# A new order at the start of a gated cross-attention kernel: second variances ahead, VectorE scales four tiles, x turned inside V's third product

## The reference

```python
x = x + tanh(g_xattn) * xattn(layernorm(x), ctx, mask, ...)
x = x + tanh(g_ffn) * ffn(layernorm(x), ...)
# xattn(h, ctx): 32 heads of 128
q = (rmsnorm(h) * ln_w) @ w_q.T ; k = ctx @ w_k.T ; v = ctx @ w_v.T
p = softmax(where(mask, q @ k.T + bias, -inf)) ; out = h + (p @ v) @ w_out.T
# ffn(h): h @ base_W.T plus 2 of 28 rank-8 experts, chosen by h @ gate_W.T
```

## Time and profile before

| | |
|---|---|
| median of 3 runs | 825.04 us |
| profiled execution, its own time | 824.99 us |
| its span | 823.2 us |
| TensorE busy | 812.8 us, 99% |
| VectorE, ScalarE, GpSimd busy | 592.9, 389.3, 454.0 us |

### The profile page before, as it was taken

One profiled execution on the slowest core, in us unless ns is written; L12 is line 12 of the kernel. 1 busy time (PEld: TensorE's weight loads), 2 busy tenths in 40 slices (PEclk: granted clock), 3 DMA queues, 4 the chain that ended last, 5 costly groups with the idle time before them and its releaser, 6 DMA issues.

```text
span 823.2 us, 14190 instructions
## 1 busy us (share of the span) xinstructions
PE 812.8 (99%) x4198; PEld 694.3 (84%) x4198; DVE 592.9 (72%) x1003; ACT 389.3 (47%) x1059; POOL 454.0 (55%) x418
## 2 busy tenths in 40 slices
PE   9979999999999999999999999999999999999998
PEld 8868888887878888888888888888888888888887
DVE  6796556766775445996888778877887788778752
ACT  6954444445222424565445634563555355545410
POOL 2465666666388383757754575457545754574200
PEclk9999999999999999999999999999999999999999
DMA  9457545454543835797566556655665565555002
GB/s 319 142 182 254 174 155 165 153 162 158 179 179 116 293 129 179 236 259 264 161 211 227 180 165 213 219 180 165 219 210 182 166 226 207 179 184 179 1 27 77
DMA packets 79102, 149.70 MB, mean 182 GB/s; under 512 B 8032, under 2 KB 42336, under 8 KB 77024
## 3 DMA queue, kind: packets, MB, share of 16 engines
q1 hardware_dynamic: 79072, 149.32, 54.4%
HBM read 97.91 MB, written 51.38 MB: 181 GB/s over the span
## 4 chain that ended last, share of the span: by engine, by line
PE 91%; DVE 4%; ACT 2%; POOL 1%; DMA 1%; issue 1%; SPq 0%; DVEq 0%; POOLq 0%; ACTq 0%
PE proj_ps L2075 18%; PE proj_ps L1895 13%; PE proj_ps L2137 11%; PE proj_ps L2156 8%; PE score_ps L1895 6%; PE proj_ps L1945 5%; PE score_ps L2156 4%; PE score_ps L1914 3%; PE proj_ps L2341 2%; PE pv_ps L2137 2%; PE turn_ps L2137 2%; PE pv_ps L2156 2%; PE turn_ps L2156 2%; PE pv_ps L1914 2%; PE turn_ps L1914 2%; PE score_ps L1945 1%
## 5 line engine op out<-in xcount | busy, mean ns | idle before, releaser
L664 POOL TENSOR_TENSOR comb<-mask_add,bias_sb 128x1024 f32<-128x1024 f32 x32 | 78.3, 2468 | 145.1 <-DVE attn L1642 145.1
L906 ACT ACTIVATE attn<-attn,neg_max 128x128 f32<-128x128 f32 x256 | 99.2, 390 | 37.8 <-DVE neg_max L1631 37.7
L1161 ACT ACTIVATE w_hi<-w_raw 128x256 fp32r<-128x256 f32 x105 | 40.0, 413 | 100.1 <-POOL w_raw L755 75.2
L765 POOL TENSOR_TENSOR w_lo<-w_raw,w_hi 128x256 fp32r<-128x256 f32 x105 | 74.4, 751 | 1.8 <-ACT w_hi L1161 1.8
L1664 DVE TENSOR_TENSOR acc<-proj_ps,acc 128x512 f32<-128x512 f32 x70 | 48.1, 689 | 35.6 <-PE proj_ps L1895 35.6
L717 POOL TENSOR_TENSOR w_lo<-w_raw,w_hi 128x256 fp32r<-128x256 f32 x64 | 49.9, 783 | 25.1 <-ACT w_hi L1021 24.9
L1895 PE MATMUL proj_ps<-w_hi,tf_hi 128*128 128x512 f32 x156 | 61.1, 392 | 0.0
L1895 PE MATMUL proj_ps<-w_hi,tf_lo 128*128 128x512 f32 x156 | 60.7, 389 | 0.0
L1895 PE MATMUL proj_ps<-w_lo,tf_hi 128*128 128x512 f32 x156 | 60.7, 389 | 0.0
L660 POOL TENSOR_TENSOR w_lo<-w_raw,w_hi 128x1024 fp32r<-128x1024 f32 x19 | 45.7, 2410 | 16.1 <-ACT w_hi L892 16.1
L1457 DVE TENSOR_TENSOR w_lo<-w_raw,w_hi 128x256 fp32r<-128x256 f32 x48 | 35.2, 738 | 24.5 <-ACT w_hi L1016 24.1
(11 more groups left out here) (414 smaller groups left out, 2526.9 us busy)
## 6 DMA issues: line engine op xcount, KB each, us to landing
w_raw<-in_weights SPq DMA_DIRECT2D x50, 512.0 KB, 5.6
q_spill<-attn SPq DMA_DIRECT2D x64, 256.0 KB, 3.1
qt<-q_spill SPq DMA_DIRECT2D x16, 1024.0 KB, 4.8
v_sb<-v_spill SPq DMA_DIRECT2D x32, 512.0 KB, 3.8
block_spill<-block_sb SPq DMA_DIRECT2D x30, 512.0 KB, 3.5
attn<-block_spill SPq DMA_DIRECT2D x120, 128.0 KB, 3.0
w_raw<-in_v_weights SPq DMA_DIRECT2D x18, 512.0 KB, 4.4
v_spill<-v_sb SPq DMA_DIRECT2D x16, 512.0 KB, 4.8
```

Source lines behind the costliest of these rows:

```text
L664: pool.tensor_tensor(comb[:, j, :, :], mask_add[:, :, :], bias_sb[:, j:j + 1, :].to_broadcast([P, B, S]), ALU.add).then_inc(comb_done, 1)
L765: pool.tensor_tensor(columns(w_lo, slot, n), raw, columns(w_hi, slot, n).bitcast(F32), ALU.subtract).then_inc(k_lo, 1)
L906: e = act.activation(probs[:, u, i, :], probs[:, u, i, :], ACT.Exp, bias=neg_max[:, u, i:i + 1], accum_out=row_sum[:, u, i:i + 1])
```

## The change

- GpSimd: the second root comes right behind the first, ahead of V's third rest, which no longer waits for the first shift; the sums for Q's pass 1 wait for three T rests instead of one product; kt's first rest moves from before pass 14 to behind the passes; the last V sums of group 0 move ahead of the fourth V weight sum of group 1.
- VectorE: the second variances come right behind the first shift; the second shift ahead of `norm_x(1)` to `(3)`; it scales tiles 4 to 7 itself; rests of the turned tiles and norms alternate in pairs; two rests of Q's A forms move behind `t_raw[3]`; `t_raw[2]` moves behind `rest_t(3)` and `rest_t(1)`.
- ScalarE: it no longer scales tiles 4 to 7, and its copies come in a new order; V's first two copies of the fourth product stand ahead of the first T form.
- TensorE: tiles 4 to 7 of x are turned in pairs inside V's third product and behind it.

```diff
--- before.py
+++ after.py
@@ -690,9 +690,8 @@
             early_rest(1)
             pool.wait_ge(consts_done, 3)
             inverse_root(1, slice(0, G), 2)
-            pool.wait_ge(shift_done, 1)
+            inverse_root(2, slice(G, B), 2)
             early_rest(2)
-            inverse_root(2, slice(G, B), 2)
             pool.wait_ge(shift_done, 2)
             early_rest(3)
 
@@ -726,7 +725,7 @@
 
             def q_phase(i):
                 if isinstance(i, int) and i == 0:
-                    pool.wait_ge(q_prod, 1)
+                    pool.wait_ge(t_lo_done, 3)
                 s_forms(i + 1)
                 rest_s(i + 1, 0, 0)
                 rest_s(i + 1, 1, 1)
@@ -736,8 +735,6 @@
             q_phase(0)
             with pool.Fori(1, NQ - 2) as i:
                 q_phase(i)
-            pool.wait_ge(kt_hi_done, 1)
-            pool.tensor_tensor(kt_form_at(1, 0), kt_raw[0], kt_form_at(0, 0).bitcast(F32), ALU.subtract).then_inc(kt_lo_done, 1)
             q_phase(NQ - 2)
 
             def rest_kt(n, place):
@@ -809,6 +806,8 @@
                 wait_v_lo(pool, g, 1)
                 pool.tensor_tensor(v_raw(g, R21), v_raw(g, R22), v_raw(g, R11), ALU.subtract).then_inc(v_sums, 1)
                 if g < VE:
+                    v_last_sums(g - 1)
+                if g < VE:
                     pool.wait_ge(vw_in[R12], 16 * (g + 1))
                 else:
                     wait_v_lo(pool, g, 2)
@@ -822,13 +821,15 @@
                     pool.wait_ge(v_post, g * VPOSTS + 9 + m)
                     pool.tensor_tensor(v_w[:, m, 0:VN[g]], v_w[:, m, 0:VN[g]], v_t[g][:, m, 0:VN[g]], ALU.add).then_inc(v_last, 1)
 
+            rest_kt(0, 1)
             rest_kt(1, 2)
             for g in range(1, VG):
                 if g >= VE:
                     v_rest(g, 0)
                 v_first_sums(g)
                 v_rest(g, 1)
-                v_last_sums(g - 1)
+                if g >= VE:
+                    v_last_sums(g - 1)
                 v_second_sums(g)
                 if g == 1:
                     pool.wait_ge(kt_lo_done, TF)
@@ -966,7 +967,7 @@
 
             def layer(i):
 
-                act.wait_ge(shift_done, i // G + 1)
+                act.wait_ge(shift_done, 1)
                 act.activation(acc[:, i, :], acc[:, i, :], ACT.Identity, bias=shift[:, i:i + 1], scale=root[:, 0, i:i + 1]).then_inc(acc_done, 1)
 
             early_half(0)
@@ -996,20 +997,17 @@
             act.activation(tanh_g[:, :], gates[:, :], ACT.Tanh).then_inc(tanh_done, 1)
             for i in range(G):
                 lead_xt(i)
-            layer(4)
-            layer(5)
+            raw_xt(0)
+            raw_xt(1)
             early_copy(2, 0)
-            raw_xt(0)
-            layer(6)
-            raw_xt(1)
-            early_copy(2, 1)
-            layer(7)
             raw_xt(2)
             raw_xt(3)
+            early_copy(2, 1)
+            lead_xt(4)
+            lead_xt(5)
             early_copy(2, 2)
             early_copy(2, 3)
-            lead_xt(4)
-            lead_xt(5)
+
             def lead_a(i, n, j, k):
 
                 wait_q_raw(act, i)
@@ -1027,24 +1025,21 @@
 
             act.wait_ge(ve_prod, 3 * VTILES)
             lead_a(0, 0, 0, 0)
+            lead_xt(6)
+            lead_xt(7)
+            early_copy(3, 0)
+            early_copy(3, 1)
+            lead_t(0)
+            lead_s(0, 0)
+            lead_s(0, 1)
+            lead_s(0, 3)
+            lead_s(0, 2)
             lead_a(0, 1, 0, 1)
             lead_a(0, 2, 1, 1)
-            lead_xt(6)
-            act.wait_ge(ve_prod, 2 * VTILES)
-            lead_s(0, 0)
-            lead_xt(7)
-            lead_t(0)
-            lead_s(0, 1)
-            early_copy(3, 0)
-            early_copy(3, 1)
             lead_t(1)
-            lead_s(0, 3)
-            lead_s(0, 2)
-            act.wait_ge(proj_done, UNITS)
             lead_t(3)
             early_copy(3, 2)
             early_copy(3, 3)
-            act.wait_ge(ve_prod, 4 * VTILES)
             lead_t(2)
 
             def lead_kt(n, place):
@@ -1420,21 +1415,24 @@
             x_stats(2)
             ordered(x_stats(3))
             layer_shift(1, first)
+            x_variances(1)
             rest_ctx(0, 1)
             rest_ctx(1, 1)
             dve.wait_ge(small_in, 48)
             norm_x(0)
-            norm_x(1)
             rest_ctx(2, 1)
             rest_ctx(3, 1)
-            norm_x(2)
-            norm_x(3)
-            x_variances(1)
             layer_shift(2, second)
-            for i in range(G):
+            for i in range(1, G):
+                norm_x(i)
+            dve.wait_ge(shift_done, 2)
+            for i in range(G, B):
+                dve.tensor_scalar(acc[:, i, :], acc[:, i, :], root[:, 0, i:i + 1], shift[:, i:i + 1], ALU.mult, ALU.add).then_inc(acc_done, 1)
+            for i in range(0, G, 2):
                 rest_xt(i, xt_hi_done, xt_lo_done, xn_ps)
-            for i in range(G, B):
-                norm_x(i)
+                rest_xt(i + 1, xt_hi_done, xt_lo_done, xn_ps)
+                norm_x(G + i)
+                norm_x(G + i + 1)
 
 
             def tile_ps(i, k):
@@ -1467,8 +1465,6 @@
             rest_xt(4, xt_hi_done, xt_lo_done, xn_ps)
             rest_xt(5, xt_hi_done, xt_lo_done, xn_ps)
             rest_a(0, 0, 0, 0)
-            rest_a(0, 1, 0, 1)
-            rest_a(0, 2, 1, 1)
             first_difference(6)
             first_difference(7)
             for i in range(G, B):
@@ -1477,9 +1473,11 @@
             rest_t(0, 1)
             dve.wait_ge(t_done, 2 * G)
             dve.tensor_tensor(t_raw[3], xt_raw[:, 2:4, half(0)], t_raw[1], ALU.subtract).then_inc(t_done, 1)
-            dve.tensor_tensor(t_raw[2], t_raw[1], xt_raw[:, 0:2, half(0)], ALU.subtract).then_inc(t_done, 1)
+            rest_a(0, 1, 0, 1)
+            rest_a(0, 2, 1, 1)
             rest_t(3, 3)
             rest_t(1, 2)
+            dve.tensor_tensor(t_raw[2], t_raw[1], xt_raw[:, 0:2, half(0)], ALU.subtract).then_inc(t_done, 1)
             rest_xt(6, xt_hi_done, xt_lo_done, xn_ps)
             rest_xt(7, xt_hi_done, xt_lo_done, xn_ps)
             rest_t(2, 4)
@@ -2050,15 +2048,16 @@
             for i in range(G):
                 turn_xn(i)
             pe.wait_ge(ve_lo, 2)
-            for m in range(VTILES):
-                early_tile(2, m)
+            early_tile(2, 0)
+            early_tile(2, 1)
             turn_xn(4)
             turn_xn(5)
-            pe.wait_ge(ve_lo, 3)
-            early_tile(3, 0)
+            early_tile(2, 2)
+            early_tile(2, 3)
             turn_xn(6)
             turn_xn(7)
-            for m in range(1, VTILES):
+            pe.wait_ge(ve_lo, 3)
+            for m in range(VTILES):
                 early_tile(3, m)
 
             a_forms = [[columns(w, WQ, n) for n in range(AF)] for w in (w_hi, w_lo)]
```

## The result

The changed kernel takes 828.5 us (median of 6 runs, 827.97 to 829.57) against 825.24 us (824.33 to 826.55). The ratio is 1.0037, 95% interval 1.0024 to 1.005: some 3 us slower, and clear of noise. Its profiled execution took 827.97 us for a span of 826.1, 2.9 more than before.

What follows compares the result with a forecast made beforehand. TensorE, busy 99%, was taken as the bound, its third product of Q waiting behind lead_t(2) and t_raw[2]. Terms 3.6 - 0.5 + 0.5 = +3.6 on 825.04 gave 828.6 us; eight-of-ten range 825.2 to 831.4.

Steps and rivals of the forecast that it cites:

- (f): T sums on VectorE: t_raw[2] ends at 53.7, Q's third product starts at 55.4 against 51.77, +3.6 us.
- (b): norm_x(1) to (3) behind the shift: held by GpSimd's subtraction (+2.2); TensorE stands 1.3 + 0.25 us turning x.
- rival 1: norm_x takes no turns with GpSimd: third product at 53.8, total 827.0 us; chance 0.25.
- (a): Second variances and root early: rest_ctx pair ends at 27.3, TensorE loses at most 0.1 us.
- (c): VectorE scales tiles 4 to 7: 0.35 us each, 1.4 for four; upper end 0.66 each, adding 1.1.
- (j): Half-speed clock after the longer wait before Q's third product: between 0 and +1.6, taken as +0.5 us.
- (h): kt's first rest moved behind the last S forms: TensorE's stand at 192.67 goes, -0.5 us.
- (i): v_last_sums(0) ahead of the last V sum: GpSimd's total to 236.5 and the 0.9 us wait unchanged, 0.
- rival 3: VectorE wins the turns against GpSimd: t_raw[2] ends before 50.0, third product at 51.5, 824.7 us; chance 0.10.
- rival 4: Both TensorE waits at Q's start go, as if lnw copy weren't behind lead_t(2): 818.3 us; chance 0.06.
- Rival 2: GpSimd's root takes turns with VectorE too: TensorE stands 1.6 us at its third key piece, 830.1 us; chance 0.17.

Runs made afterwards that it cites:

- e1: Changed kernel with one line moved: VectorE's third T sum, t_raw[2], back directly behind t_raw[3]; 824.22 us, 0.9989 of the kernel before.
- e2: Changed kernel with ScalarE's copy of Q's first product ahead of lead_t(2), the sum t_raw[2] left late; 824.66 us, 0.9994 of the kernel before.
- e7: Changed kernel with GpSimd's fourth early rest waiting for six norms instead of the second shift; 825.61 us, 1.0012 of the kernel before.
- e8: Changed kernel with 26 unused identity matmuls filling TensorE's wait between Q's second and third product; 825.41 us, 1.0020 of the kernel before.
- e5: Kernel before with only kt's first rest moved from before pass 14 to behind the passes on GpSimd; 823.50 us, ratio 0.9988.
- e6: Kernel before with only group 0's last V sums moved ahead of group 1's fourth weight sum on GpSimd; 822.39 us, ratio 0.9977.
- e10: Changed kernel, third sum late, with e3's copy order, e7's wait, and pass 0's fifth sum ahead of pass 1's rests; 821.28 us, 0.9948 of the kernel before.
- e3: Changed kernel with ScalarE's copy of Q's first product behind lead_t(1), the second's ahead of lead_t(2); 825.78 us, 1.0005 of the kernel before.
- e11: e10 with the three rests of pass 0's A forms on GpSimd instead of VectorE; 821.57 us, 0.9957 of the kernel before.
- e9: Changed kernel with the edits of e1 and e7 together; 822.95 us, 0.9971 of the kernel before.
- e4: Changed kernel with 52 unused identity matmuls between Q's second and third product, overrunning the wait; 832.06 us, 1.0076 of the kernel before.

## Why the prediction was right

The forecast was 828.6 us; 828.5 was measured. The mechanism held: one long wait before the third product, with its copy behind the late sum. That the total came out within 0.1 us is luck. Of the terms, the start and the clock cost 1.3 us more than said, two stretches further on gave back 1.8 that the sum had at nothing, and the balance of the profiles is +2.9 and that of the medians +3.3, against +3.6.

- **(f), the term of +3.6.** From rest_t(0)'s start to t_raw[2]'s end were to be 8.6 us; the rows have 45.91 to 54.49, 8.58. GpSimd's four rests (46.26) fall into it and take their turns as worked out. From the sum to the third product 1.74 was said, and 1.73 it is. e1 and e2 show that this order is the cause.
- **(b), the forecast against rival 1.** norm_x was taken at the upper end (+2.2): three took 4.20 us where three alone take 2.07 (e7). TensorE's two waits for them come to 1.1 us, but they cost more than that: from the first turned tile to Q's first product it took 16.45 us (30.40 to 46.85) and in e7 14.47 (29.96 to 44.43), so 2.0 were lost, where 1.55 was said.
- **(a) failed in size.** TensorE was to lose 0.1 us at the third key piece and stood 0.8. GpSimd's root took 2.01 us instead of 1.65 and V's third rest behind it 2.58 instead of 2.40, so that this rest ended at 26.90 instead of 26.1, and rest_ctx(2) and (3), which stood beside it, at 28.05 instead of 27.3. norm_x(0) also had to wait for the gates' transfer until 23.89, which the prediction did not have; as the pair stood until GpSimd had ended, no run shows that this cost anything. With (b), Q's first product came at 46.85 instead of 46.0 and rest_t(0) at 45.91 instead of 45.1: 0.8 late, and so +4.45 at the third product instead of +3.6. Why the root was longer was not tested.
- **(c)** Scaling took 0.46 a tile, between the ends of 0.35 and 0.66, 0.4 us more for the four than taken. What that cost TensorE was not measured.
- **(j)** TensorE ran at 1.2 GHz for 5.2 us behind the wait, which cost 2.5 in this profile, 0.9 more than before, against +0.5 taken (e8 leaves the size in the median open). The row of the changed kernel (us, busy of PE, PEld, DVE, ACT, POOL, granted clock, DMA share, GB/s):

```profile
55.00:62.00 7.00, 5.79 (x15) 4.61 (x16) 3.27 (x5) 3.43 (x8) 4.04 (x5) 0.54 0.33 126
```

- **(h)** held: VectorE's sum is back to its length alone (changed kernel), against 3.43 in the earlier trace rows, and e5 gains 1.0 where 0.5 was said, within its interval.

```profile
191.47 1.22 DVE L1519 TENSOR_TENSOR block_sb<-block_sb,comb 128x1024 f32<-128x1024 f32 x1
```

- **(i) is the step that was wrong in kind**: "GpSimd's total to 236.5 is unchanged, and so is the 0.9 us wait". The total is unchanged, but ScalarE's hi copy, on which that wait hangs, follows the third weight sum. In the kernel before (ScalarE, then GpSimd) and in the changed one (GpSimd, ScalarE, VectorE):

```profile
234.06 1.06 ACT L1064 ACTIVATE w_hi<-w_raw 128x1024 fp32r<-128x1024 f32 x1 [9.91 <-PE proj_ps L2156]
```

```profile
231.56 2.40 POOL L810 TENSOR_TENSOR w_raw<-w_raw 128x1024 f32<-128x1024 f32 x1
```

```profile
231.48 2.41 POOL L807 TENSOR_TENSOR w_raw<-w_raw 128x1024 f32<-128x1024 f32 x1
...
233.98 1.06 ACT L1059 ACTIVATE w_hi<-w_raw 128x1024 fp32r<-128x1024 f32 x1 [5.12 <-POOL w_raw L807]
...
236.63 2.10 DVE L1495 TENSOR_TENSOR w_lo<-w_raw,w_hi 128x1024 fp32r<-128x1024 f32 x1
```

Before, the copy was put down to TensorE, but GpSimd's sum ended at 233.96, 0.1 us ahead of it: it was the real releaser, and the kernel's text has ScalarE wait for that sum (`v_sums`) there. TensorE comes to that place 4.7 us later after the change and this copy does not, so the wait is gone. e6, with this edit alone, shows the wait gone as well.

The terms as measured in the two profiles: +4.45 (said +3.6), clock +0.9 (+0.5), 192 us -0.6 (-0.5), 237 us -1.1 (0), later -0.7 (0). **Rival 1** is out by e7, **rival 3** by the turns seen, **rival 4** by the wait itself. **Rival 2** is out too, though the sign that the prediction named for it, a wait of TensorE at its third key piece, did show (0.8 us, see (a)): the two ct_lo beside the root took 1.29 us, no more than alone, and it was the root that took longer. The Trainium skill ("SBUF — State Buffer", Who interferes with whom) says that a VectorE instruction with two SBUF inputs contends with a GpSimd instruction that reads SBUF, and norm_x does so here (4.20 against 2.07). A hold for the whole length, which the prediction took over for all such pairs and the page words for VectorE's 2-port modes, does not show for the root of 8 columns: it ran from 22.33 to 24.34 and would have held the second ct_lo, and did not.

## What to carry to other kernels

When an operation is moved later because its own reader is late, read down the list of the engine that consumes it: here the third sum was not urgent (e10 keeps it late), but the copy of a bank stood behind its hi part. Order each in-order list by who waits for the next entry, and where an early entry has to wait, move the urgent ones ahead of it (e10). Where the wait of an engine is put down to one releaser, look for another that ended in the same tenth of a microsecond before calling a move free.

## What the runs showed of the hardware that was not expected

- Scaling 128x512 in place by VectorE with two scalars per partition takes 0.46 us a tile with GpSimd idle (changed kernel, 32.76); a subtraction of two 128x512 tiles takes 0.60 (22.16).
- A matmul of a 128x128 float32 identity counts as two records of 0.11 us (26 issued, 52 recorded in 5.97 us; 52 issued, 104 recorded in 11.77), and the granted clock stayed at 1.00 through them and behind them.
- With the same list of TensorE up to there, the half-clock stretch began at the end of the wait for the third product in the kernel before (51.6), at the end of the first product in e5 (47.5) and within it in e6 (46.9), and their third product then waited 1.1 and 0.8 us instead of 2.3. In e2, whose longest wait there was 1.8 us, and in e3, e10 and e11 the granted clock was 1.00 throughout. Where the slow stretch falls, and whether it comes, differs from one profiled execution to the next; what a change wins by it is read from medians.
- A wait of TensorE for the blocks' transfer near 375 us shows in some profiles (0.3 us in e6, 0.4 in e2, 0.6 in e10, 1.3 in e9 and in e4) and not in others. As e4, the slowest kernel, has it at 1.3, it does not come of an early start alone; its cause was not looked for.
